# Windowed attention in half tiles of four heads: a new order of TensorE's work, other PSUM banks, and q and k projected earlier

## What is computed

```python
x = _L0_cond(x)                      # clip(scores, 0, 1) * v, then @ Wo.T
for each of 2 layers:
    h = shift_token(x)               # second half of the features from the token before
    q, k, v = split(h @ wqkv)        # 8 heads of 64
    q, k = l2norm(q) * qs, l2norm(k) * ks
    q, k = rotary_xpos(q, k)
    sim = 8 * q @ k.T                # each token sees the 256 before it and itself
    x = x + softmax(sim, masked) @ v @ wo
    h = layernorm(shift_token(x)) * lg + lb
    a, g = split(h @ w1 + b1)
    x = x + (a * gelu(g)) @ w2 + b2
```

## Time and profile before

| | |
|---|---|
| median of 3 runs | 3343.11 us (3342.11 to 3343.95) |
| profiled execution | 3346.07 us |
| its span | 3343.9 us |
| TensorE busy | 3223.4 us, 96% |
| VectorE busy | 1709.5 us, 51% |
| ScalarE busy | 1441.8 us, 43% |
| GpSimd busy | 909.4 us, 27% |
| mean granted TensorE clock | 0.985 |
| chain that ended last, TensorE's share | 94% |

### The profile page before, as it was taken

The page is one execution under the profiler, slowest core; times in us unless marked ns, Lnnn a source line. Parts: engine busy times, 40 slices in busy tenths (PEclk is TensorE's granted clock), DMA queues, the critical chain, the costliest instruction groups (busy, mean ns, idle before and its releaser), DMA issues.

```text
span 3343.9 us, 53165 instructions
## 1 busy us (share of the span) xinstructions
PE 3223.4 (96%) x19592; PEld 2634.2 (79%) x19592; DVE 1709.5 (51%) x3549; ACT 1441.8 (43%) x2941; POOL 909.4 (27%) x1542
## 2 busy tenths in 40 slices
PE   7998999999996999999999999999995999999999
PEld 6996888888875888888877888888884888788887
DVE  4555666666665333333323666666665433334342
ACT  1115777777772111111113777777774111111111
POOL 3105444454436000000034544444443400000000
PEclk9999999999997999999999999999997999999999
DMA  4311111111114110011131111111113211111110
GB/s 164 120 67 36 64 58 61 61 58 64 55 52 117 38 38 19 20 38 38 38 114 37 58 64 61 58 43 51 61 52 86 82 51 45 51 51 51 51 38 20
DMA packets 149794, 194.82 MB, mean 58 GB/s; under 512 B 23286, under 2 KB 90998, under 8 KB 149284
## 3 DMA queue, kind: packets, MB, share of 16 engines
q1 hardware_dynamic: 133172, 174.64, 16.0%
q10 hardware_dynamic: 16368, 16.78, 1.5%
HBM read 120.06 MB, written 41.95 MB: 48 GB/s over the span
## 4 chain that ended last, share of the span: by engine, by line
PE 94%; DVE 2%; issue 1%; ACT 1%; POOL 1%; DMA 0%; SPq 0%; DVEq 0%; POOLq 0%; ACTq 0%
PE bank L333 30%; PE bank L335 27%; PE bank L334 27%; PE bank L743 5%; PE bank L563 3%; PE bank L818 1%; DVE a_PT_lo L1295 0%; ACT a_PT_hi L1015 0%; DMA c_headmask<-headmask_const 0%; ACT a_P L1010 0%; DVE f_h L1400 0%; PE bank L571 0%; PE bank L581 0%; DVE f_hraw L1408 0%; ACT f_hT_hi L1088 0%
## 5 line engine op out<-in xcount | busy, mean ns | idle before, releaser
L333 PE MATMUL bank<-f_hT_hi,f_w_hi 128*128 128x512 f32 (+1 forms) x1408 | 557.2, 396 | 16.9 <-ACT f_hT_hi L1088 15.5
L335 PE MATMUL bank<-f_hT_hi,f_w_lo 128*128 128x512 f32 (+1 forms) x1408 | 553.6, 393 | 0.0
L1107 ACT ACTIVATE f_gate<-bank,f_b 128x512 f32<-128x512 f32 (+1 forms) x176 | 121.2, 689 | 1000.7 <-PE bank L335 1000.7
L334 PE MATMUL bank<-f_hT_lo,f_w_hi 128*128 128x512 f32 (+1 forms) x1408 | 552.6, 393 | 0.0
L1436 DVE SCALAR_TENSOR_TENSOR f_uraw<-bank,f_b,f_gate 128x512 f32<-128x512 f32 (+1 forms) x176 | 132.1, 750 | 754.3 <-ACT f_gate L1107 754.1
L1010 ACT ACTIVATE a_P<-a_S,a_bias 128x384 f32<-128x384 f32 x512 | 310.9, 608 | 252.8 <-DVE a_bias L1285 252.8
L1285 DVE CUSTOM_DVE_ANT_0 a_S<-bank,a_masks,a_q 128x384 f32<-128x384 f32 x512 | 295.1, 614 | 64.5 <-issue 47.6
L333 PEld LDWEIGHTS bank<-f_hT_hi,f_w_hi 128*128 128x128 f32 (+1 forms) x1408 | 261.3, 186 | 78.7 <-ACT f_hT_hi L1088 15.9
L333 PE MATMUL bank<-a_PT_hi,a_V_hi 128*64 128x128 f32 x1536 | 301.8, 232 | 16.1 <-DVE a_PT_lo L1295 16.1
L335 PEld LDWEIGHTS bank<-f_hT_hi,f_w_lo 128*128 128x128 f32 (+1 forms) x1408 | 260.9, 185 | 64.5
L334 PEld LDWEIGHTS bank<-f_hT_lo,f_w_hi 128*128 128x128 f32 (+1 forms) x1408 | 261.3, 186 | 62.7
(11 more groups left out here) (164 smaller groups left out, 6882.7 us busy)
## 6 DMA issues: line engine op xcount, KB each, us to landing
a_h<-x_layer_in SPq DMA_DIRECT2D x128, 128.0 KB, 2.3
a_res<-x_layer_in SPq DMA_DIRECT2D x64, 256.0 KB, 2.8
x_after_attention<-out_tiles SPq DMA_DIRECT2D x64, 256.0 KB, 2.0
f_res<-x_after_attention SPq DMA_DIRECT2D x64, 256.0 KB, 3.5
f_stage<-in_L_ffn_w SPq DMA_DIRECT2D x60, 256.0 KB, 3.5
f_h<-x_after_attention ACTq DMA_DIRECT2D x28, 512.0 KB, 4.3
c_x<-in_x SPq DMA_DIRECT2D x32, 256.0 KB, 2.9
x_layer_in<-out_tiles SPq DMA_DIRECT2D x32, 256.0 KB, 2.0
```

The lines of the kernel that those rows point to most:

```text
L333: pe.matmul(dst, w[0], m[0], start=start, stop=False)
L334: pe.matmul(dst, w[0], m[1], start=False, stop=False)
L335: return pe.matmul(dst, w[1], m[0], start=False, stop=stop)
L1107: act.activation(f_gate[0:ROWS[m], m % 2, :], bank[pair_of(u, m, end) + 1][0:ROWS[m], :], ACT.Gelu, bias=f_b1[0:ROWS[m], 1, m:m + 1]).then ...
```

## The change

A step has two halves of four heads each. The first half has the products of P and V of the last four heads of tile t-1, the scores of heads 4 to 7 of tile t, P's transposes of the first pair, the projection V, P's transposes of the second pair, the output projection, then the transposes of q and k of tile t+1. The second half has the products of the first four heads of tile t, the scores of heads 0 to 3 of tile t+1, P's transposes of pair 2, the projection K, those of pair 3, the projection Q, and the transposes of h.

The scores use banks 0 to 3, and inside a group the even and the odd head take turns pass by pass. Bank 0 (`spare`) is lent to the projection of Q and to that of the output; bank 7 has K and V. The products of P and V go to bank 4, P's transposes to banks 5 and 6, which the transposes of q, k and h use between them. P's high and low halves have four slots. The two slots of masked scores become two tensors, and small tensors move in SBUF. The lists of ScalarE and VectorE are put in a matching order; GpSimd's list is unchanged.

```diff
+        GROUPS = PAIRS // 2
+        work, spare, o_bank, q_turn, k_turn = bank[7], bank[0], bank[4], bank[5], bank[6]
+        h_turn = lambda x: bank[6] if x < 2 else bank[5]
+        q_work = lambda x: work if x == 0 else spare
...
@@ tensor: waits
                 def h_T(x):
-                    if x >= 2:
-                        pe.wait_ge(a_KT_hi, START + G + x - 1)
-                        pe.wait_ge(a_KT_lo, START + G + x - 1)
+                    if x >= 3:
+                        pe.wait_ge(a_PT_lo, START + (G + x - 2) * PAIRS)
                 def q_T(x):
                     pe.wait_ge(a_q_rotated, START + G + x + 1)
+                        pe.wait_ge(a_PT_lo, START + (G + x - 1) * PAIRS + 2)
                 def k_T(x):
                     pe.wait_ge(a_k_normed, START + G + x + 1)
-                    pe.wait_ge(a_QT_hi, START + G + x + 1)
-                    pe.wait_ge(a_QT_lo, START + G + x + 1)
...
                 def q_project(x):
+                        pe.wait_ge(a_S_masked, START + (G + x - 1) * H + 1)
+                    project(0, x, q_work(x), a_q_mm)
                 def project_out(x):
+                        pe.wait_ge(a_S_masked, START + (G + x + 1) * H + H // 2 + 1)
...
+                def scores(x, g):
+                        if x >= 2:
+                            pe.wait_ge(a_out_set, START + G + x - 1)
+                    elif here(x + 1):
+                        pe.wait_ge(a_q_copied, START + G + x + 2)
+                        pe.wait_ge(a_q_squared, START + G + x + 2)
+                    pe.wait_ge(a_S_masked, START + (G + x) * H + g * H // 2)
+                    for i in (2 * g, 2 * g + 1):
+                        for step, (q_part, k_part) in enumerate(((0, 0), (0, 1), (1, 0))):
+                            for odd in range(2):
+                                r = slice(odd * HD, odd * HD + HD)
+                                mm = pe.matmul(bank[2 * (i % 2) + odd][:, 0:WIN * P], a_QT[q_part][r, x % 2, i, :],
+                                               a_KT[k_part][r, i, j * P:(j + WIN) * P], start=(step == 0), stop=(step == 2))
...
                 def p_T(x, i):
+                    if i == 0 and here(x + 2) and x >= 0:
+                        pe.wait_ge(a_hT_lo, START + G + x + 3)
+                    if i == 2 and here(x + 1):
+                        pe.wait_ge(a_QT_lo, START + G + x + 2)
+                        pe.wait_ge(a_KT_lo, START + G + x + 2)
+                def pv(x, g):
+                    pe.wait_ge(a_O_lo, START + 2 * (GROUPS * (G + x) + g))
+                    pe.wait_ge(a_PT_lo, START + (G + x) * PAIRS + 2 * g + 2)
```

More of the change, by code:

```diff
@@ L115, in adaln_ffn_program @@
         out_tiles = sb("out_tiles", [P, 2, D])
-        bank = [ctx.enter_context(nc.psum_tensor(f"bank{i}", [P, 512], F32)) for i in range(2)]
-        pt_banks = ctx.enter_context(nc.psum_tensor("bank23", [P, 2, 512], F32))
+        bank = [ctx.enter_context(nc.psum_tensor(f"bank{i}", [P, 512], F32)) for i in range(5)]
+        pt_banks = ctx.enter_context(nc.psum_tensor("bank56", [P, 2, 512], F32))
         bank += [pt_banks[:, 0, :], pt_banks[:, 1, :]]
-        bank += [ctx.enter_context(nc.psum_tensor(f"bank{i}", [P, 512], F32)) for i in range(4, 8)]
+        bank += [ctx.enter_context(nc.psum_tensor("bank7", [P, 512], F32))]
         with ExitStack() as st:
@@ L651, in attention @@
                 G = l * TILES
-                turn, work = bank[6], bank[7]
                 def h_T(x):
@@ L678, in project @@
                     for k in range(KT_):
-                        mm = three_passes(pe, work[:], [a_hT[i][:, x % 2, k, :] for i in range(2)],
+                        mm = three_passes(pe, dst[:], [a_hT[i][:, x % 2, k, :] for i in range(2)],
                                           [a_w[which][i][:, k, :] for i in range(2)], k == 0, k == KT_ - 1)
@@ L713, in project_out @@
                     for k in range(PAIRS):
-                        mm = three_passes(pe, work[:], [a_OT[i][:, k, :] for i in range(2)],
+                        mm = three_passes(pe, spare[:], [a_OT[i][:, k, :] for i in range(2)],
                                           [a_w[3][i][:, k, :] for i in range(2)], k == 0, k == PAIRS - 1)
                     mm.then_inc(a_wo_mm, 1)
-                def scores(x, i):
+                def scores(x, g):
                     j = x % QUAD
-                    if i == 0:
+                    if g == 0:
                         if x == 0:
@@ L730, in scores @@
                             pe.wait_ge(ready, START + G + x + 1)
[L731 to L736, removed]
+                        if x >= 2:
[10 more added lines that the diff above has]
+                                               a_KT[k_part][r, i, j * P:(j + WIN) * P], start=(step == 0), stop=(step == 2))
+                                if step == 2:
+                                    mm.then_inc(a_S_mm, 1)
                 def p_T(x, i):
@@ L989, in value, with o_hi @@
                     act.activation(a_V[0][:, x % QUAD + WIN - 1, :], work[:], ACT.Copy).then_inc(a_V_hi, 1)
-                def o_hi(x):
-                    if x == 0:
+                def o_hi(x, g):
+                    if x == 0 and g == 0:
                         for j in range(QUAD):
                             act.wait_ge(f_stored[j], START + l * (BLOCKS * 16))
-                    act.wait_ge(a_PV_mm, START + (G + x + 1) * PAIRS)
+                    act.wait_ge(a_PV_mm, START + GROUPS * (G + x) + g + 1)
+                    heads = o_bank[0:HD, :].rearrange("p (i o n) -> p i o n", i=2, o=2)
                     for odd in range(2):
-                        act.activation(a_OT[0][odd * HD:odd * HD + HD, :, :], quarters(bank[4 + odd][0:HD, :]), ACT.Copy)\
+                        act.activation(a_OT[0][odd * HD:odd * HD + HD, 2 * g:2 * g + 2, :], heads[:, :, odd, :], ACT.Copy)\
                            .then_inc(a_O_hi, 1)
@@ L1058, in body @@
                             normalize(t, 3)
+                        if here(t):
+                            o_hi(t, 0)
+                            p_T(t, 2)
+                        if here(t + 1):
+                            exp(t + 1, 0)
+                            exp(t + 1, 1)
                         if here(t + 2):
@@ L1336, in body @@
                         if here(t):
-                            inverse(t, 2)
                             p_T(t, 1)
+                            inverse(t, 3)
                         if here(t + 1):
-                            q_T(t + 1)
                             k_norm(t + 1)
@@ L1355, in body @@
                             mask_max(t + 1, 1)
+                        if here(t):
+                            p_T(t, 2)
+                        if here(t + 1):
+                            mask_max(t + 1, 2)
+                            mask_max(t + 1, 3)
                             inverse(t + 1, 0)
+                        if here(t + 2):
+                            sums(1, t + 2)
                         if here(t):
                             p_T(t, 3)
+                        if here(t + 1):
+                            inverse(t + 1, 1)
                         if here(t + 3):
```

212 lines of the change are left out of this document (97 added, 115 removed).

## The result

| | before | after |
|---|---|---|
| median | 3342.61 us (3341.86 to 3343.95, 4 runs) | 3408.69 us (3407.13 to 3410.04, 4 runs) |
| ratio | | 1.0197 (95%: 1.0183 to 1.0210) |
| profiled execution, span | 3346.07, 3343.9 us | 3407.38, 3405.2 us |
| one steady tile | 23.07 us | 23.99 us |

What follows compares the result with a forecast made beforehand. TensorE, busy throughout a 23.07 us tile, would instead wait on a loop through ScalarE and GpSimd: 16.38 and 7.50, 23.9 us a tile. With the ends, +22 per layer, +44 on 3346: 3390 us; 8-in-10 range 3350 to 3440.

Steps and rivals of the forecast that it cites:

- TensorE's list: TensorE's own work in a steady attention tile: 22.5 us (22.1 to 23.0), 0.57 less than 23.07.
- products of P and V with their entry into the scores: TensorE, steady tile: products stay at 4.48 us; entering the scores behind them, twice, adds 0.20.
- scores: TensorE, steady tile: two groups of twelve score matmuls at 1.25 us, 2.50 for 2.92 before.
- projections: TensorE, steady tile: all four now end before transposes, 11.48 us for 11.88 before.
- transposes: TensorE, steady tile: 36 transposes in six stretches, 3.84 us.
- The chain: Steady-tile loop: 16.38 us from K's end through ScalarE, GpSimd and VectorE to k's transposes, then 7.50 on TensorE; 23.9.
- The waits: TensorE, steady tile: second scores wait about 0.4 us for q's copy, k's transposes about 1.1 for k's norm.
- The order of the heads: Score groups: even and odd head in turn costs nothing, since the two heads already run at the same time.
- The clock: Rival, chance 0.15: waits lower TensorE's clock, 1.2 to 1.6 us in a third to all of 60 tiles; 3415 to 3480.
- The ends of a layer: Each layer's attention: start +2 us (21.3 to 23.3), end -4 (33.2 to 29.2).

Runs made afterwards that it cites:

- experiment 5: Changed kernel, q's squares and copy ahead of the normalizations, output's high halves ahead of the second normalizations, two norm rounds instead of three: 3289.41 us, 0.9846 to before.
- experiment 9: Changed kernel, ScalarE reordered (q's copy, output's high halves earlier), three norm rounds, k's rotation addition on VectorE at the second half tile's end: 3290.60 us, 0.9848 to before.
- experiment 2: Changed kernel with two instead of three rounds of the iteration in GpSimd's norms: 3329.30 us, 0.9963 to the kernel before.
- experiment 6: Changed kernel with four instead of three rounds of the iteration in GpSimd's norms: 3554.87 us, 1.0636 to the kernel before.
- the first: Changed kernel with q's squares and copy moved ahead of both normalizations and h's copy in ScalarE's list: 3332.31 us, 0.9968 to the kernel before.
- experiment 3: Kernel before the change with two instead of three rounds of the iteration in GpSimd's norms: 3339.95 us, 0.9990 to the kernel before.
- experiment 7: Kernel before the change with four instead of three rounds of the iteration in GpSimd's norms: 3350.72 us, 1.0027 to the kernel before.
- experiment 4: Changed kernel with each head's three score passes issued one after the other instead of even and odd head in turn: 3405.24 us, 1.0190 to the kernel before.

## Why the prediction was right

**TensorE's list.** Forecast 22.5 us a tile without waits, measured 22.13 in experiments 5 and 9. By terms: products of P and V with their entry into the scores 4.68 forecast and 4.67 measured (2.33 and 2.34); scores 2.50 and 2.52; projections 11.48 and 11.38; transposes 3.84 and 3.56, the term that was mis-sized most. Part of that is the sum itself: the pieces that the prediction uses later, four times 0.60 and three times 0.44, make 3.72, and 3.84 follows from no row. The rest is that transposes ahead of products end as early as those ahead of a projection (k's and h's four take 0.36 each). The half tiles do shorten TensorE's list, by 0.94 us and not by 0.57.

**The chain.** Forecast 16.38 from K's end to k's transposes and 7.50 on TensorE, 23.9; measured 16.49 and 7.50, 23.99. ScalarE was given 6.56 to the end of q's copy and took 6.65. The waits: 0.4 and 1.1 forecast, 0.53 and 1.05 in the trace. Experiments 2 and 6 move the period by what they take or add (1.27 less and, where the clock holds, 1.28 more for 1.30 us in the norms); the first takes 2.50 out of the chain and gets 1.32, because GpSimd's chain is next. Experiments 3 and 7 show that the chain had a reserve before: 1.30 us more in the norms costs 0.1 a tile there. The 0.37 us by which TensorE's list was mis-sized lie mostly outside the 7.50 of the loop and so never reached the time. The result's time could not test that term, since the list sets no tile there; experiments 5 and 9 do.

**The order of the heads.** Costed at nothing, and experiment 4 confirms it.

**The clock.** It had a chance of 0.15 and didn't come in the steady tiles. The price of 1.2 to 1.6 us fits the 1.47 of experiment 6. Its upper end of 3480 should be 3486 by its own terms (60 times 1.6 on 3390).

**The ends of a layer.** Here the forecast failed. It gave +2 for a start and -4 for an end of each layer, -4 in all; measured is +7.3 (-0.2, +3.8, +2.3, +1.4). The two starts come to the forecast +4 only by luck. The first attention began 3.8 us earlier, for the condition layer ended at 246.5 instead of 250.3; the change leaves that layer's lists alone, and the first transposes of k vary from 267.7 to 271.7 over these runs. The start itself, from the first to the second transposes of k, took 24.9 instead of 21.3, and in the second layer, from the projection of V on, it also lost 3.6. With 54.1 in place of 47.8 for the 60 tiles this makes 61.3 instead of 44 between the spans. The end went wrong most. From the last transposes of k to the last output projection I laid out 29.2 us; it took 37.9 (33.2 before). Counted to the end of that projection the loss is only 2.4, 40.9 against 38.5, which fits the +2.3: the projection itself took 5.3 at about half clock before and 3.0 now.

```profile
1019.32:1024.61 5.29, 5.29 (x12) 3.78 (x12) 0.00 (x0) 0.00 (x0) 0.00 (x0) 0.53 0.00 0
1051.87:1054.85 2.98, 2.98 (x12) 2.15 (x12) 0.00 (x0) 0.00 (x0) 0.00 (x0) 1.00 0.00 0
```

The first of these lines is the kernel before, the second the changed one. TensorE of the changed kernel in order of time:

```profile
1013.96 0.66 PE L567 MATMUL bank<-ident,a_krot 128*128 128x128 f32 x4 [1.05 <-DVE a_krot L1262]
...
1020.82 0.85 PE L762 MATMUL bank<-ident,a_P 128*128 128x128 f32 x6 [1.99 <-DVE a_PT_lo L1307]
...
1032.66 1.13 PE L762 MATMUL bank<-ident,a_P 128*128 128x128 f32 x6 [1.98 <-DVE a_PT_lo L1307]
...
1042.86 1.09 PE L762 MATMUL bank<-ident,a_P 128*128 128x128 f32 x6 [2.17 <-DVE a_PT_lo L1307]
...
1051.87 0.47 PE L337 MATMUL bank<-a_wo_hi,a_OT_hi 128*128 128x512 f32 x1 [1.86 <-DVE a_OT_lo L1314]
```

The step's projections used to fill the time between two pairs of P; at the end there are none, so each pair waits 2 us for the pair before. These waits I had, at 1.9. What I had not counted is the lower clock in the work between them:

```profile
1023.20:1030.00 6.80, 6.35 (x50) 5.90 (x51) 1.84 (x5) 3.27 (x8) 0.00 (x0) 0.52 0.40 110
1033.43:1036.83 3.40, 3.40 (x11) 2.71 (x10) 1.36 (x5) 3.00 (x8) 0.00 (x0) 0.55 0.01 2
```

In the first of these stretches 36 products took 4.00 instead of 2.33 and twelve scores 2.15 instead of 1.27, in the second the output projection 4.24 instead of 2.84. With the last 36 products (4.07, from 1045.94) such stretches hold some 6 of the 8.7 us that were missing; the rest is P's transposes with their round trips and the output's last halves, 1.86 instead of 1.2. I had written that rival down for the steady tiles and forgotten it where wait follows wait. The starts are another case: between the first and the second transposes of k TensorE waits 8.1 us in the first layer and 6.6 in the second, where it waited 1.0 and 1.4 before. The forecast had 1.4 of these, and not the 2.67 of the second scores for q's copy, the 2.0 of q's transposes for P's low parts and, in the first layer, 1.60 of k's for its norm. No run changed the starts or the ends alone; that part stays a reading of the trace.

## What to carry to other kernels

When an order on the bounding engine is shortened, lay out the longest chain that leaves it and comes back, with everything that stands ahead of each link in the in-order lists of the other engines, and compare its length with the new period: an engine with 5.7 idle us a tile, as ScalarE here, can still be the one that sets it. The gain is real only after the links are put in the order of their lateness, and behind the first chain stands the next one (ScalarE's list, then GpSimd's, then one addition on VectorE). "It waits there anyway" has to be read as a time interval, since work that begins at the end of the wait is all on the path.

## What the runs showed of the hardware

- The clock at repeated waits: one wait of 1.05 us and one of 0.53 in each 24 us left the granted clock at 1.00 through the steady part; one of 2.34 a tile was followed by a stretch at 0.50 in 43 of 60 tiles, each 1.47 us longer, and by 1.00 in the others; a single one of 2.67 was followed by 9.4 us at 1.00.
- Two heads' score matmuls on different halves of the rows ran 0.45 us side by side whether they were issued in turn or three and three.
- A group of scores in the 64-row form cost about 0.2 us besides its steps (a step is one matmul of each of two heads): six matmuls took 0.73 us, twelve 1.27, so a step 0.18. The projection ahead of it took 0.12 more than one ahead of transposes (2.98 and 2.86), 36 products ahead of it 0.08 more than twice 18 ahead of transposes (2.33 and 1.13).
